# New instruction orders for the 16-head attentions and the ternary feed-forward of a four-layer block

## The reference

```python
q = (query @ Wq + bq)              # 16 heads of 16; query = layernorm(x)
k, v = key_value @ Wk + bk, key_value @ Wv + bv      # 120 context rows of 192
attn = softmax(clip(q k^T * 16**-0.5, -1e4, 1e4))    # the clip only in the first attention
x = x + (attn @ v) @ Wo + bo

h = bit_linear(layernorm(x), w1)   # x rounded to 8 bits by row, w to -1, 0, 1
h = silu(depthwise_conv1d(h))      # 3 taps along the 256 rows
x = x + bit_linear(h, w2)          # h rounded to 8 bits by row, again
```

## Time and profile before

| what | value |
|---|---|
| median of 3 runs | 5412.2 µs (5409.13 to 5420.22) |
| the profiled execution's own time | 5421.46 µs |
| its span | 5419.7 µs |
| busy: PE, PEld, DVE, ACT, POOL | 87%, 67%, 59%, 36%, 34% |
| stage a0, about | 9 to 834 µs of the span |
| stage f0, about | 834 to 1413 µs |
| stage a2, about | 2449 to 2995 µs |

### The profile page before, as it was taken

One profiled execution on the slowest core, in us unless ns is written; L12 is line 12 of the kernel. 1 busy time (PEld: TensorE's weight loads), 2 busy tenths in 40 slices (PEclk: granted clock), 3 DMA queues, 4 the chain that ended last, 5 costly groups with the idle time before them and its releaser, 6 DMA issues. The chain is left out here.

```text
span 5419.7 us, 92076 instructions
## 1 busy us (share of the span) xinstructions
PE 4706.9 (87%) x32476; PEld 3648.8 (67%) x32476; DVE 3212.5 (59%) x9943; ACT 1968.3 (36%) x4118; POOL 1828.6 (34%) x2246
## 2 busy tenths in 40 slices
PE   6777775777789969997999699999999977999978
PEld 4555553555678858885777588888888844777845
DVE  4666655777665523316887377777777753444344
ACT  3333332454444413213555233334333323222234
POOL 2111112444325523305554033333333221565522
PEclk8888887999889979998999899999999988999989
DMA  3444541111342132212221211001100027222223
GB/s 92 108 105 99 115 96 52 50 51 46 117 152 56 50 78 75 67 48 78 77 69 55 71 31 34 29 29 31 35 30 29 25 71 240 86 94 88 78 91 108
DMA packets 329715, 397.17 MB, mean 73 GB/s; under 512 B 66021, under 2 KB 289995, under 8 KB 318507
## 3 DMA queue, kind: packets, MB, share of 16 engines
q1 hardware_dynamic: 315946, 366.04, 23.7%
q0 software_dynamic: 13312, 25.25, 2.0%
HBM read 297.64 MB, written 93.55 MB: 72 GB/s over the span
## 5 line engine op out<-in xcount | busy, mean ns | idle before, releaser
L2527 PE MATMUL fa_h<-fa_xnT,fa_w 128*128 128x256 f32 x2048 | 485.8, 383 | 0.0
L2539 PE MATMUL fa_y<-fa_w,fa_hT 128*128 128x256 f32 x2048 | 462.5, 379 | 0.0
L2539 PEld LDWEIGHTS fa_y<-fa_w,fa_hT 128*128 128x128 f32 x2048 | 386.8, 190 | 65.0 <-issue 14.8
L2527 PEld LDWEIGHTS fa_h<-fa_xnT,fa_w 128*128 128x128 f32 x2048 | 382.5, 191 | 71.2 <-issue 13.2
L2406 ACT ACTIVATE fa_hT<-fa_h,fa_b 128x256 f32<-128x256 f32 x512 | 215.0, 471 | 544.5 <-PE fa_h L2527 482.6
L423 DVE TENSOR_REDUCE a_mx<-a_score 128x16 f32<-128x1920 f32 x128 | 276.0, 2157 | 59.1 <-PE a_score L607 59.1
L128 POOL TENSOR_SCALAR a_rs<-a_mv 128x2 f32<-128x2 f32 x96 | 21.3, 222 | 728.5 <-DVE a_mv L122 725.1
L657 PE MATMUL a_av<-a_pT,a_vp 120*32 120x256 f32 x2048 | 183.2, 420 | 90.9 <-DVE a_qa L437 90.9
L2913 ACT ACTIVATE m_hT<-m_h,m_b 128x256 f32<-128x256 f32 x256 | 107.5, 471 | 403.8 <-PE m_h L2950 403.8
L1553 PE MATMUL r_h<-r_xnT,r_rw 128*128 128x256 f32 x1024 | 246.7, 389 | 0.7 <-ACT r_xnT L1503 0.7
L1908 PE MATMUL e_h<-e_xT,e_w 128*128 128x256 f32 x1024 | 234.3, 383 | 2.5 <-DVE e_xT L1707 2.5
(11 more groups left out here) (451 smaller groups left out, 11300.3 us busy)
## 6 DMA issues: line engine op xcount, KB each, us to landing
a_floor<-a_lowest SPq DMA_DIRECT2D x64, 960.0 KB, 9.8
cv_toep<-kernels SPq DMA_DIRECT2D x16, 2048.0 KB, 9.5
x<-a_xo SPq DMA_DIRECT2D x96, 256.0 KB, 4.0
f_xb<-x SPq DMA_DIRECT2D x64, 256.0 KB, 2.8
f_xres<-x SPq DMA_DIRECT2D x64, 256.0 KB, 2.9
a_xb<-x SPq DMA_DIRECT2D x64, 256.0 KB, 3.0
e_w<-in_L_ffn_ew SPq DMA_DIRECT2D x16, 1024.0 KB, 7.2
a_cb<-in_ctx SPq DMA_DIRECT2D x96, 90.0 KB, 2.0
```

The costliest lines, as they stand in the source:

```text
L2527: last = pe.matmul(h_ps[j % 2][:, c, :], w1[:, e, k, f:f + P], xnT[it.p][:, k, :], start=k == 0, stop=k == KD - 1)
L2539: last = pe.matmul(bank[:, t * D:(t + 1) * D], hT[e % 2][:, k, t * P:(t + 1) * P], w2[:, e, k, :], start=k == 0, stop=k == KE - 1)
```

## The change

Only the order of the steps within a slot changes, with two lags; and one small tile gets four buffers.

- a0: `put_max` moves from lag 4 at the head of DVE's slot to lag 3 near its end, behind `clips(1)`; `low_out` goes from lag 4 at the head of ACT's slot to lag 3 between `exps(0)` and `exps(1)`, and `exps(0)` goes behind `q_out` and `k_out`; on PE `turn_max` goes in front of `shifted_scores(1)`; on DVE `norm` in front of `weigh`.
- f0: new lists on all four engines. On DVE `y_out` and `hidden_max(0)` end the slot, and `quantise` stands in front of `h_out(3)`. On POOL `scale_hidden` goes from lag 6 at the head to lag 5 behind `spread` of the hidden scale, in the same slot. On PE `down` stands in front of `conv(0)` as before, and `turn` goes between `up(0)` and `up(1)`. `hinv` has four buffers.
- a2: on PE `scores(1)` goes in front of `project_k`; on DVE `combine` goes from lag 2 behind `reciprocals` to lag 1 behind `norm`, and `norm_stats` goes behind `maxima(1)`.

```diff
 heads_attention, vector, clip:
-                    (4, put_max), (3, maxima(0)), (5, reciprocals), (4, clips(0)), (1, norm_stats), (3, maxima(1)), (5, weigh),
-                    (1, norm), (4, clips(1)), (5, y_out)], **RUN)
+                    (3, maxima(0)), (5, reciprocals), (4, clips(0)), (1, norm_stats), (3, maxima(1)), (1, norm), (5, weigh),
+                    (4, clips(1)), (3, put_max), (5, y_out)], **RUN)
 vector, routed:
-                pipeline(dve, B, DEPTH, later([(4, put_max), (3, maxima(0)), (5, reciprocals)]) + ([(2, combine)] if routed else []) + later([
-                    (1, norm_stats), (3, maxima(1)), (5, weigh), (1, norm), (5, y_out)]), **RUN)
+                pipeline(dve, B, DEPTH, later([
+                    (4, put_max), (3, maxima(0)), (5, reciprocals), (3, maxima(1)), (1, norm_stats), (5, weigh), (1, norm)])
+                    + [(1, combine)] + later([(5, y_out)]), **RUN)
 scalar, clip:
-                    (4, low_out), (2, xT_out), (5, raw_out), (4, exps(0)), (2, q_out), (2, k_out), (2, v_out), (4, exps(1))], **RUN)
+                    (2, xT_out), (5, raw_out), (2, q_out), (2, k_out), (4, exps(0)), (2, v_out), (3, low_out), (4, exps(1))], **RUN)
 tensor, clip:
-                    (3, scores(1)), (5, widen), (2, project_v), (4, shifted_scores(1)), (3, turn_max), (5, project_o)], **RUN)
+                    (3, scores(1)), (5, widen), (2, project_v), (3, turn_max), (4, shifted_scores(1)), (5, project_o)], **RUN)
 tensor, routed:
-                    (2, turn_x), (3, scores(0)), (5, attend(0)), (5, attend(1)), (4, shifted_scores(0)), (2, project_q), (2, project_k),
-                    (3, scores(1)), (5, widen), (2, project_v), (4, shifted_scores(1)), (5, project_o), (3, turn_max)]), **RUN)
+                    (2, turn_x), (3, scores(0)), (5, attend(0)), (5, attend(1)), (4, shifted_scores(0)), (2, project_q), (3, scores(1)),
+                    (2, project_k), (5, widen), (2, project_v), (4, shifted_scores(1)), (5, project_o), (3, turn_max)]), **RUN)
 ternary_feed_forward, gpsimd:
-                (6, scale_hidden), (5, spread(dg2, hscale, hq, HQ, dg2_ready, row2_done)), (1, roots_of),
+                (5, spread(dg2, hscale, hq, HQ, dg2_ready, row2_done)), (5, scale_hidden), (1, roots_of),
                 (2, spread(dg, ainv, quant, QN, dg_ready, row_done))], unroll=4, history=4)
 vector:
-                (4, h_out(0)), (4, h_out(1)), (6, round_hidden), (5, hidden_max(1)), (7, y_out), (4, h_out(2)), (5, hidden_scale), (1, norm_stats),
-                (4, h_out(3)), (2, quantise), (4, hidden_max(0))], unroll=4, history=4)
+                (4, h_out(0)), (4, h_out(1)), (5, hidden_max(1)), (6, round_hidden), (1, norm_stats), (5, hidden_scale), (4, h_out(2)),
+                (2, quantise), (4, h_out(3)), (7, y_out), (4, hidden_max(0))], unroll=4, history=4)
 scalar:
-                (6, quantised), (4, silu(0)), (3, turn_out), (3, row_out(aux, row, row_done, row_ready, h_ready, 4)),
-                (5, row_out(aux2, row2, row2_done, row2_ready, multiplied, 1)), (4, sizes(0)), (4, silu(1)), (4, sizes(1))], unroll=4, history=4)
+                (4, silu(0)), (3, row_out(aux, row, row_done, row_ready, h_ready, 4)), (4, sizes(0)),
+                (5, row_out(aux2, row2, row2_done, row2_ready, multiplied, 1)), (3, turn_out), (6, quantised), (4, silu(1)), (4, sizes(1))], unroll=4, history=4)
 tensor:
-                (4, up(0)), (4, up(1)), (7, down), (4, conv(0)), (5, turn_max), (4, up(2)), (3, make_row(aux, dg, dg_ready, row_done, row_ready)),
-                (3, turn), (4, up(3)), (5, make_row(aux2, dg2, dg2_ready, row2_done, row2_ready)), (4, conv(1))], unroll=4, history=4)
+                (4, up(0)), (3, turn), (4, up(1)), (7, down), (4, conv(0)), (5, turn_max), (4, up(2)), (4, up(3)),
+                (3, make_row(aux, dg, dg_ready, row_done, row_ready)), (5, make_row(aux2, dg2, dg2_ready, row2_done, row2_ready)), (4, conv(1))], unroll=4, history=4)
```

More of the change, by code:

```diff
@@ L709, in ternary_feed_forward @@
     stt, mv, rs = ([st.sb(f"{n}{p}", [P, TL, k]) for p in two] for n, k in (("st", 6), ("mv", 2), ("rs", 1)))
-    amax, ascale, ainv, hmax, hscale, hinv = ([st.sb(f"{n}{p}", [P, TL]) for p in two]
-                                              for n in ("amax", "ascale", "ainv", "hmax", "hscale", "hinv"))
+    amax, ascale, ainv, hmax, hscale = ([st.sb(f"{n}{p}", [P, TL]) for p in two]
+                                        for n in ("amax", "ascale", "ainv", "hmax", "hscale"))
+    hinv = [st.sb(f"hinv{p}", [P, TL]) for p in range(4)]
     qx = [st.sb(f"qx{p}", [P, TL, D], BF16) for p in two]
@@ L890, in hidden_scale @@
                 c.add(dve.reciprocal(hscale[p][:], hmax[p][:]))
-                dve.tensor_scalar(hinv[p][:], hmax[p][:], back[:, 1:2], None, ALU.mult)
+                dve.tensor_scalar(hinv[it.at][:], hmax[p][:], back[:, 1:2], None, ALU.mult)
                 c.wait()
@@ L904, in y_out @@
                 for t in range(TL):
-                    last = dve.scalar_tensor_tensor(xo[it.p][:, t, :], y_ps[:, t, :], hinv[it.p][:, t:t + 1],
+                    last = dve.scalar_tensor_tensor(xo[it.p][:, t, :], y_ps[:, t, :], hinv[it.at][:, t:t + 1],
                                                     xres[it.p][:, t, :], ALU.mult, ALU.add)
```

## The result

The change made the kernel slower: 5493.95 µs against 5410.66 µs of the kernel before beside it on the same chip (medians of 4 runs each), a ratio of 1.0153 with a 95% interval of 1.0133 to 1.0174, or +83.3 µs. The forecast was 5490, with a range of 5360 to 5570. The profiled execution has a span of 5498.8 µs (before: 5419.7).

The account below looks back on a forecast made before the run. The prediction took the longest closed loop of waits through the in-order lists to bound each slot, with a2 near TensorE's own work. Terms a0 -174, f0 +136, a2 +116 summed to +78 on the 5412.2 median: 5490 µs, range 5360 to 5570.

Parts of the forecast that it names:

- a2's term: In a2, slots go from 16.21 to 20.5 µs over 27 slots: +116 µs, bounds +27 and +143.
- The first loop: In a0, the new loop from one attend(0) to the next, through reciprocals, clips and put_max: 18.3 µs.
- the floor loop: In a0, a second loop from clips(0) through low_out and the floor's landing: 19.8 µs, rather 18 to 19; 18.8 taken.
- the landing: In a0, the floor's time from issue to landing: 9.8 µs by the earlier median, expected shorter with the queue to itself.
- the forecast slot of 21.3: In f0, slot with quantise held 4.7 µs by scale_hidden and conv(1) at the lower clock; +136 over 29 slots.
- the 128x2 factor: In f0, quantise's small instruction named as alternative to a rounding one for the hold of some 4.5 µs under scale_hidden.
- the other reading in the prediction: In f0, if GpSimd holds only VectorE's two-input instructions, quantise is not held and the slot is near 15.3 µs.
- the contention of `combine` with `add_bias`: In a2, combine, with two SBUF inputs, meets a_kda and add_bias behind the norm: 0.1 to 1.3 µs a slot.
- The clock's term: In a2, 2.4 to 3 µs of TensorE idle puts attend at the lower clock: +1.7 µs, 5.4 against 3.7.
- That TensorE keeps its clock: Rival, f0 and a2: conv(1) and attend keep the higher level, or a2 costs little; -11 in all, 5401 µs; chance 0.28.
- That VectorE keeps the port: Rival, f0 and a2: quantise and combine hold POOL back instead; -185, 5227 µs; chance 0.12.
- That a0 gains less: Rival, a0: late floor or lower clock, 21 µs a slot, -108; in all +144, 5556 µs; chance 0.15.

Follow-up runs that it names:

- a2_bias_first: The changed kernel with POOL in a2 doing add_bias before roots_of and spread_k: 5449.67 µs against 5405.92 of the kernel before, ratio 1.0078.
- a2_fill: The changed kernel with ten unused matmuls in front of attend(0) in a2: 5443.05 µs against 5405.92 of the kernel before, ratio 1.0071.
- a0_only: The kernel before with the new lists of a0 alone: 5257.28 µs against 5443.39 of the kernel before, ratio 0.966.
- f0_only: The kernel before with the new lists of f0 alone and the four hinv buffers: 5577.49 µs, ratio 1.0239 to the kernel before.
- a2_scores_only: The changed kernel with VectorE's old list in a2, so only TensorE's order is new there: 5334.71 µs against 5405.92 of the kernel before, ratio 0.9866.
- three_edits: The changed kernel with VectorE's old a2 list and f0's VectorE and POOL steps reordered: 5321.5 µs against 5455.84 of the kernel before, ratio 0.9754.
- a2_only: The kernel before with the new lists of a2 alone: 5577.89 µs, ratio 1.0258 to the kernel before.

## Why the prediction was right

It was right in its sign, its total and its mechanisms. That the total came within 4 µs is luck: the stages were off by −29 in a0, −7 in f0 and +39 in a2, which cancel. Luck has a part in a2's term too: it was worked out from a trace in which `attend` kept the higher level in every slot, and on another chip the same orders cost a2 +130.

**a0 (−174 forecast, −203 measured).** The first loop was summed as 18.3 and measured 18.06: 3.72 for `attend`, 1.67, 3.45 up to `maxima(1)`, 5.37 from there to `clips(1)` (forecast 5.53, with clamp and norm held to 1.00 and 1.75), 2.20 and 1.65. Inside the forecast 5.53 the norm was taken too high (+1.5, measured +1.03) and the clamp too low (+0.4, measured +0.8). The step that failed is the choice of the floor loop, 18.8, as the bound: `clips` waited 3.0 µs for it in the whole stage. Its mis-sized part is the landing, 8.8 µs in the sum, which took at most 8.2 in the slot shown (298.04 to 306.21). The slot before was 24.6 in the mean, as taken (24, and in six slots 27.4 to 28, where `clips(0)` waits 2.5 to 3.1 µs for the floor), so 30 slots of 6.5 are 195; the other 8 µs are not traced to a cause.

**f0 (+136 forecast, +129 measured).** Every term of the forecast slot of 21.3 can be read off the slot above, which is 20.48: 7.31 up to `quantise` (7.5), 1.48 before the hold (1.8), 4.49 held (4.7), 1.56 for its rest (1.4), 0.74 for `h_out(3)` (0.7), 4.90 through `conv(1)` to the next `h_out` (5.15). The slot before was also shorter, 16.1 to 16.2 in the mean where the one of the earlier trace rows has 16.62, so that the difference, 4.3 to 4.4, came out near the forecast 4.7. I had named a rounding instruction *or the 128x2 factor* as the one to be held and said the forecast would be wrong if L844 to L852 kept their durations. They did, so by that sentence this part was wrong: the held one is the clamp in front of them (L840 of the kernel before). The criterion was drawn one line too narrow, the mechanism stood. The clamp has a single input, and it took 4.49 µs against 0.17 alone; so the other reading in the prediction, that only two-input instructions are held and f0 goes down to 15.3, has fallen. The Trainium skill ("GPSIMD Engine Reference", section 8, "Key points") has GpSimd contend with VectorE's instructions in a 2-port mode or with two SBUF inputs. The trace agrees as far as it goes; in which mode the clamp ran it doesn't show.

**a2 (+116 forecast, +155 measured).** By pieces against the earlier trace rows and the slot around it: `reciprocals` to `maxima(1)` 4.91 before, 4.22 after (−0.7, as estimated); from there to the norm 2.67 and 4.49 (+1.8; forecast 1.75: `norm_stats` and the wait for the roots); norm to `y_out` 2.65 and 4.89 (+2.2; forecast 1.2 net of the wait, plus 0.1 to 1.3 of contention); `attend` +1.5. The mis-sized term is the contention of `combine` with `add_bias`: 4.3 a slot leaves 0.35 for it, near the low end of its bounds, and it was 1.1 of at most 1.3. The clock's term, 1.7, was about right in the slot shown and too small in those where `attend` took 6.6. a2_bias_first shows the first, a2_fill the second.

**The rivals.** That TensorE keeps its clock fell: `conv(1)` 4.22, `attend` 5.1 and more. That VectorE keeps the port fell: in f0 it was VectorE that waited in every slot, and POOL kept its 4.51. That a0 gains less fell with a floor that was hardly ever late (3.0 µs in the stage).

What stays open: a version with a0's change, the new TensorE order of a2 and f0 as it was wasn't run; a0_only, at 0.966, is the best that was.

## What to carry to other kernels

In a pipeline of in-order lists an edit is worth what it does to the one loop that closes last: moving a small producer, `low_out`, and its `put_max` ahead of work that doesn't need them was worth 149 µs, and moving two steps of 1.7 and 1.2 µs, `combine` and `norm_stats`, from an engine's waiting time onto that loop cost 155 with all that followed. Before an order is changed, ask of VectorE's instructions between SBUF tiles, like the norm, the clamp, the maximum and `combine` here, which GpSimd instruction will run beside them. In f0 the price was the rest of that instruction, whatever the size of the held one, and cutting GpSimd's work in pieces or moving the neighbour spread or moved the hold. And count every gap of TensorE twice, once as the wait and once as the slower matmuls behind it.

## What the runs showed that I had not expected

**The same orders, another clock.** a2 with its old lists took 16.21 µs a slot in the kernel before as profiled, with `attend` at 3.7 in every slot. In a0_only and f0_only it took 16.98, with the same idle in front of `attend`. TensorE's rows of one slot of a0_only:

```profile
2532.30 0.64 PE L657 MATMUL a_av<-a_pT,a_vp 120*32 120x256 f32 x8 [0.41 <-DVE a_qa L437]
...
2534.03 0.89 PE L657 MATMUL a_av<-a_pT,a_vp 120*32 120x256 f32 x8
2534.54 1.16 PE L660 MATMUL a_total<-a_pT,a_onesel 120*32 120x256 f32 x6
```

Eight matmuls go from 0.64 to 0.89 µs and six then take 1.16: by this the level falls in the middle of `attend`, though the gap before it was 0.41 µs. `attend` took 4.5 µs in nearly every slot. The mean granted clock of the stage hardly tells the two apart: 0.98 in both. The same pair is seen with the new TensorE order: 16.0 in a2_scores_only, 17.12 in three_edits, with identical lists in a2. The kernels with the slower a2 ran on the two chips on which the kernel before took 5443 and 5456 µs, the others where it took 5411 and 5406; a2 with VectorE's new list took 713 to 715 µs on both kinds. A kernel before made up of the untouched stages of a0_only, f0_only and a2_only (a0 825, f0 577, between 1053, a2 583, behind 2404) is 5442 long, which is what it took there. That the chip is the cause is inferred from these five traces, no kernel having been traced on both kinds of chip; why one chip holds the level through a2 and another doesn't stays open.

**A filler that leaves a gap may do nothing.** 20 unused matmuls in a gap of 7.3 µs left 2.88 and changed nothing in all slots but one, although the mean granted clock of f0 rose from 0.82 to 0.92; 31 left 0.42 and gave the higher level back. In a2 2.27 µs of idle were too much and 0.85 were not. In a0 of the kernel before, 1.76 were not too much either. And with 0.41 the level fell in a2 of a0_only. The idle time alone doesn't say which it will be; what came before and after it counts too, and these runs don't settle how.

**The held instruction may be tiny.** A clamp of 128x2 numbers waited 4.49 µs, and with GpSimd's work in eight pieces nearly every instruction of the quantise was held for a part of one.
